# The chosen experts' DRAM round trip, by halves: own writes, reads and semaphores in a mixture-of-experts chain

## The reference

```python
x = x + L0(x)   # top 2 of 8 experts per batch: (gelu(x Wg) * (x Wu)) Wd, 256 -> 1024 -> 256,
                # weighted by the renormalised softmax, plus one shared expert of the same form
x = x + L1(x)   # x times a mix of 8 masked 256x256 matrices, mixed per batch, plus bias
x = x + L2(x)   # base matrix plus rank-16 terms of 8 experts
x = x + L3(x)   # the one argmax expert per batch: (silu(x Wu + b) * (x Wg + b)) Wd + b
```

## Time and profile before

| what | value |
|---|---|
| median of 3 runs | 1282.7 us (1278.59 to 1284.48) |
| the profiled execution's own time | 1279.28 us |
| its span in the trace | 1277.7 us |
| mean granted clock of TensorE | 0.965 |
| busy: PE / DVE / ACT / POOL | 1157.5 / 719.9 / 431.1 / 466.0 us |
| DMA | 245.07 MB in 267302 packets, mean 192 GB/s |

### The profile page before, as it was taken

One profiled execution on the slowest core, in us unless ns is written; L12 is line 12 of the kernel. 1 busy time (PEld: TensorE's weight loads), 2 busy tenths in 40 slices (PEclk: granted clock), 3 DMA queues, 4 the chain that ended last, 5 costly groups with the idle time before them and its releaser, 6 DMA issues.

```text
span 1277.7 us, 24975 instructions
## 1 busy us (share of the span) xinstructions
PE 1157.5 (91%) x6894; PEld 971.0 (76%) x6895; DVE 719.9 (56%) x1255; ACT 431.1 (34%) x845; POOL 466.0 (36%) x296
## 2 busy tenths in 40 slices
PE   8999997987967998797987797998999999899998
PEld 7999985775755776665765576787999999788776
DVE  6766675546646557465564555654555655544443
ACT  4456521322312222222322222232223223366664
POOL 2377686007126018044080636201000000688750
PEclk9999999998989999899998999998999999899999
DMA  7288858567666657657676677555655546576753
GB/s 215 72 281 300 310 149 276 160 208 195 169 209 191 198 180 208 208 162 240 188 209 200 181 211 221 160 165 151 177 145 143 136 130 192 176 251 217 216 165 106
DMA packets 267302, 245.07 MB, mean 192 GB/s; under 512 B 79936, under 2 KB 241984, under 8 KB 265152
## 3 DMA queue, kind: packets, MB, share of 16 engines
q1 hardware_dynamic: 253520, 193.95, 50.3%
q0 software_dynamic: 13680, 49.81, 13.2%
HBM read 176.59 MB, written 67.11 MB: 191 GB/s over the span
## 4 chain that ended last, share of the span: by engine, by line
PE 52%; DMA 22%; SPq 9%; DVE 7%; issue 6%; ACT 2%; POOL 1%; DVEq 0%; ACTq 0%; POOLq 0%
DMA squares<-acc 11%; DMA routing<-squares 10%; PE bank L765 7%; PE bank L766 7%; PE bank L767 7%; PE bank L1199 6%; DVE RS L1835 3%; PE bank L1228 3%; PE bank L855 3%; SPq L314 2%; PE bank L1043 2%; PE bank L906 2%; PE bank L908 2%; PE bank L1177 2%; PE bank L907 2%
## 5 line engine op out<-in xcount | busy, mean ns | idle before, releaser
L611 POOL TENSOR_TENSOR W<-raw,one 128x1024 fp32r<-128x1024 f32 x79 | 150.5, 1905 | 649.3 <-DVE acc L1902 354.4
L765 PE MATMUL bank<-W,RS 128*128 (+1 forms) x512 | 214.0, 418 | 54.7 <-DVE RS L1795 52.3
L855 PE MATMUL bank<-W,RS 128*128 x480 | 186.4, 411 | 39.7 <-DVE RS L1835 39.3
L766 PE MATMUL bank<-W,RS 128*128 (+1 forms) x512 | 208.4, 407 | 0.0
L1289 ACT ACTIVATE FS<-bank 128x512 f32<-128x512 f32 (+1 forms) x200 | 115.2, 576 | 274.2 <-PE bank L767 244.5
L767 PE MATMUL bank<-W,RS 128*128 (+1 forms) x512 | 207.5, 405 | 0.0
L613 POOL TENSOR_TENSOR W<-raw,W 128x1024 fp32r<-128x1024 f32 x79 | 195.3, 2472 | 6.2
L1835 DVE TENSOR_TENSOR RS<-routing,RS 128x512 fp32r<-128x512 f32 x120 | 123.7, 1068 | 85.8 <-ACT RS L1303 85.3
L765 PEld LDWEIGHTS bank<-W,RS 128*128 128x128 f32 x512 | 101.2, 198 | 86.5 <-issue 65.5
L1303 ACT ACTIVATE RS<-routing 128x512 fp32r<-128x512 f32 x120 | 70.3, 625 | 236.0 <-DMA routing<-squares 226.6
L855 PEld LDWEIGHTS bank<-W,RS 128*128 128x128 f32 x480 | 91.7, 191 | 71.9 <-issue 57.6
(11 more groups left out here) (236 smaller groups left out, 2072.5 us busy)
## 6 DMA issues: line engine op xcount, KB each, us to landing
raw<-in_w POOLq DMA_DIRECT2D x87, 512.0 KB, 4.8
acc<-in_w SPq DMA_DIRECT2D x70, 512.0 KB, 5.3
routing<-squares SPq DMA_DIRECT2D x60, 512.0 KB, 3.9
mixes<-acc SPq DMA_DIRECT2D x16, 1024.0 KB, 6.3
W<-mixes SPq DMA_DIRECT2D x16, 1024.0 KB, 6.1
squares<-X SPq DMA_DIRECT2D x60, 256.0 KB, 3.5
squares<-acc SPq DMA_DIRECT2D x60, 256.0 KB, 3.5
FS<-in_xT SPq DMA_DIRECT2D x200, 64.0 KB, 3.0
```

The lines of the kernel that those rows point to most:

```text
L611: pool.tensor_tensor(hi, raw[:, k, :], ones_like(PIECE), ALU.mult).then_inc(done, 1)
L765: pe.matmul(ps, ah, bh, start=(i == 0), stop=False)
L766: pe.matmul(ps, ah, bl, start=False, stop=False)
L855: mm = pe.matmul(both, chunk(hh[h], c), w2_, start=(h == 0 and c == 0), stop=(h == 1 and c == 3))
```

## The change

The tensor `squares` gets a place for each half, and `hidT` becomes two tiles' worth of columns, one for each half. Each half has its own write, its own read, and its own semaphores `square_out[h]` and `hidT_in[h]`. The transpose (s, h) waits for the write (s-1, h) alone. Nothing else is computed, and the same bytes travel.

SyncE's order in step s becomes: x for s+2; write (s, 0); read (s-1, 1); the mixed group's weights where there are any; write (s, 1); read (s, 0); the store of s-2. ScalarE takes the high part (s-1, 0) ahead of gelu (s, 1), and (s-1, 1) behind it. VectorE takes the low part (s-1, 0) ahead of hidden (s, 1), and (s-1, 1) at the end, behind the add. At the end of the stage TensorE does down (67, 1) one shared quarter later.

```diff
-    squares = nc.dram_tensor("squares", (2, P, I0), F32, kind="Internal").ap()
+    squares = nc.dram_tensor("squares", (2, 2, P, I0 // 2), F32, kind="Internal").ap()
...
-        hidT = routing[:, 0:I0]
+        hidT = [routing[:, I0 // 2 * h:I0 // 2 * (h + 1)] for h in range(2)]
...
+            def write_square(s, p, h, at):
+
+                n = P if at.half is None else S
+                sp.wait_ge(squared, 2 * s + h + 1)
+                sp.dma_start(squares[p, h].rearrange("p (g x) -> p g x", g=4)[:, :, 0:n],
+                             square[h][:, 0:4 * n].rearrange("p (g x) -> p g x", g=4)).then_inc(square_out[h], 16)
+
+            def read_hidT(s, p, h, at):
+
+                n = P if at.half is None else S
+                sp.wait_ge(square_out[h], 16 * s + 16)
+                sp.dma_start(hidT[h].rearrange("p (a x) -> p a x", a=4)[:, :, 0:n],
+                             squares[p, h].rearrange("(a i) (g x) -> (i g) a x", a=4, g=4)[:, :, 0:n])\
+                    .then_inc(hidT_in[h], 16)
...
             with sp.Fori(0, NMIXED0) as m:
                 for k in range(BODY):
-                    s, at = 2 + BODY * m + k, place_at(m, k - 2)
-                    if at.half != 0:
-                        load_skill(S0 + s + 2, k % 2, place_at(m, k + 2))
+                    s, p = 2 + BODY * m + k, k % 2
+                    at, before = place_at(m, k), place_at(m, k - 1)
+                    load_skill(S0 + s + 2, p, place_at(m, k + 2))
+                    write_square(s, p, 0, at)
+                    read_hidT(s - 1, 1 - p, 1, before)
                     if k < 2:
                         load_mixed0(m, 0, ((0, 1, 2, 3), (4, 5))[k], S0 + BODY * m)
                     if k in (HALVES[0] + 3, HALVES[0] + 4):
                         load_mixed0(m, 1, ((0, 1, 2, 3), (4, 5))[k - HALVES[0] - 3], S0 + BODY * m + HALVES[0] + 3)
-                    write_squares(s, k % 2, place_at(m, k))
-                    if at.half != 0:
-                        store_chosen(S0 + s - 2, k % 2, at)
-                    else:
-                        load_skill(S0 + s + 2, k % 2, place_at(m, k + 2), added=S0 + s - 1)
-                    read_hidT(s, k % 2, place_at(m, k))
+                    write_square(s, p, 1, at)
+                    read_hidT(s, p, 0, at)
+                    if place_at(m, k - 2).half != 0:
+                        store_chosen(S0 + s - 2, p, place_at(m, k - 2))
...
-            for q in range(2):
-                up_gate_late(0, 0, q)
-                last = load_expert_at(NR0 - 2 + q)
-                for h in range(2):
-                    down_chosen(NR0 - 2 + q, h, last)
+            up_gate_late(0, 0, 0)
+            last = load_expert_at(NR0 - 2)
+            for h in range(2):
+                down_chosen(NR0 - 2, h, last)
+            up_gate_late(0, 0, 1)
+            last = load_expert_at(NR0 - 1)
+            down_chosen(NR0 - 1, 0, last)
             up_gate_late(0, 0, 2)
+            down_chosen(NR0 - 1, 1, last)
...
-                act.wait_ge(hidT_in, 16 * s + 16)
+                act.wait_ge(hidT_in[h], 16 * s + 16)
...
+                if before_at is not None:
+                    hidden_hi_chosen(s - 1, 0, before_at)
                 gelu(1, 2 * g + 1, n=n)
                 if before_at is not None:
-                    for h in range(2):
-                        hidden_hi_chosen(s - 1, h, before_at)
+                    hidden_hi_chosen(s - 1, 1, before_at)
...
                 if not (isinstance(s, int) and s == 0):
-                    dve.wait_ge(squares_out, 32 * s)
+                    dve.wait_ge(square_out[h], 16 * s)
...
+                if before_at is not None:
+                    hidden_lo_chosen(s - 1, 0, before_at)
                 hidden_chosen(s, 1, at)
                 hidden_squares(s, 1, at)
...
-                for h in range(2):
-                    hidden_lo_chosen(s - 1, h, before_at)
                 if add_at is not None:
                     add(g - 2, p, add_at)
+                hidden_lo_chosen(s - 1, 1, before_at)
```

More of the change, by code:

```diff
@@ L252, in build @@
         hh_done, hl_done = sem("hh_done"), sem("hl_done")
-        squared, squares_out, hidT_in = sem("squared"), sem("squares_out"), sem("hidT_in")
+        squared = sem("squared")
+        square_out = [sem(f"square_out{h}") for h in range(2)]
+        hidT_in = [sem(f"hidT_in{h}") for h in range(2)]
         down_done, acc_done, add_step = sem("down_done"), sem("acc_done"), sem("add_step")
@@ L297, in turned_hid @@
         def turned_hid(h):
-            return hidT.rearrange("p (a h k t) -> p h k a t", a=4, h=2, k=4)[:, h]
+            return hidT[h].rearrange("p (a k t) -> p k a t", a=4, k=4)
         def turned_mixed(h, c):
-            return hidT.rearrange("p (a y) -> p a y", a=4)[:, :, S * h + 32 * c:S * h + 32 * (c + 1)]
+            return hidT[h].rearrange("p (a x) -> p a x", a=4)[:, :, 32 * c:32 * (c + 1)]
         block = ctx.enter_context(nc.Block())
@@ L363, in load_shared, with load_skill @@
                 home_x(g - 2)
-            def load_skill(g, p, at, added=None):
+            def load_skill(g, p, at):
                 slot = 2 * at.full if at.half is None else 2 * FULL0 + 2 * at.mixed
                 batches = table_values(sp, source[0:1, bass.ds(slot, 2)], NB - 1)
-                if added is None:
-                    sp.wait_ge(xl_done, g - 1)
-                else:
-                    sp.wait_ge(acc_done, added)
+                sp.wait_ge(xl_done, g - 1)
                 load_x(g, p, batches)
@@ L418, in _ @@
             spill(WPIECES - 1)
-            def write_squares(s, p, at):
-                n = D if at.half is None else P
-                for h in range(2):
[L423 to L435, removed]
+            def write_square(s, p, h, at):
[3 more added lines that the diff above has]
+                             square[h][:, 0:4 * n].rearrange("p (g x) -> p g x", g=4)).then_inc(square_out[h], 16)
@@ L437, in _ @@
+            def read_hidT(s, p, h, at):
[4 more added lines that the diff above has]
+                    .then_inc(hidT_in[h], 16)
             for k in range(NSTAGE):
                 sp.wait_ge(spilled[k], 16 * WPIECES // NSTAGE)
-            write_squares(0, 0, FIRST_TWO[0])
@@ L440, in _ @@
             load_skill(S0 + 2, 0, place_at(0, 0))
-            read_hidT(0, 0, FIRST_TWO[0])
+            write_square(0, 0, 0, FIRST_TWO[0])
+            write_square(0, 0, 1, FIRST_TWO[0])
+            read_hidT(0, 0, 0, FIRST_TWO[0])
             load_skill(S0 + 3, 1, place_at(0, 1))
-            write_squares(1, 1, FIRST_TWO[1])
-            read_hidT(1, 1, FIRST_TWO[1])
+            write_square(1, 1, 0, FIRST_TWO[1])
+            read_hidT(0, 0, 1, FIRST_TWO[0])
+            write_square(1, 1, 1, FIRST_TWO[1])
@@ L445, in _ @@
+            read_hidT(1, 1, 0, FIRST_TWO[1])
             with sp.Fori(0, NMIXED0) as m:
                 for k in range(BODY):
-                    s, at = 2 + BODY * m + k, place_at(m, k - 2)
-                    if at.half != 0:
-                        load_skill(S0 + s + 2, k % 2, place_at(m, k + 2))
+                    s, p = 2 + BODY * m + k, k % 2
[3 more added lines that the diff above has]
+                    read_hidT(s - 1, 1 - p, 1, before)
@@ L453, in _, with load_late @@
                         load_mixed0(m, 1, ((0, 1, 2, 3), (4, 5))[k - HALVES[0] - 3], S0 + BODY * m + HALVES[0] + 3)
-                    write_squares(s, k % 2, place_at(m, k))
-                    if at.half != 0:
-                        store_chosen(S0 + s - 2, k % 2, at)
-                    else:
-                        load_skill(S0 + s + 2, k % 2, place_at(m, k + 2), added=S0 + s - 1)
-                    read_hidT(s, k % 2, place_at(m, k))
-            def load_late(t):
-                for k in range(2):
+                    write_square(s, p, 1, at)
+                    read_hidT(s, p, 0, at)
+                    if place_at(m, k - 2).half != 0:
+                        store_chosen(S0 + s - 2, p, place_at(m, k - 2))
+            def load_late(t, ks=(0, 1)):
+                for k in ks:
                     sp.wait_ge(xl_done, S1 + 2 * t + k - 1)
@@ L470, in store_x3 @@
                              x3out.rearrange("p (t d) -> p t d", t=2)).then_inc(x3_stored, 16)
-            load_late(0)
-            write_squares(NR0 - 2, 0, LAST_TWO[0])
-            store_chosen(S1 - 4, 0, place(NR0 - 4))
-            read_hidT(NR0 - 2, 0, LAST_TWO[0])
-            write_squares(NR0 - 1, 1, LAST_TWO[1])
+            load_late(0, (0,))
+            write_square(NR0 - 2, 0, 0, LAST_TWO[0])
+            read_hidT(NR0 - 3, 1, 1, place(NR0 - 3))
+            write_square(NR0 - 2, 0, 1, LAST_TWO[0])
+            read_hidT(NR0 - 2, 0, 0, LAST_TWO[0])
+            store_chosen(S1 - 4, 0, place(NR0 - 4))
+            load_late(0, (1,))
+            write_square(NR0 - 1, 1, 0, LAST_TWO[1])
+            read_hidT(NR0 - 2, 0, 1, LAST_TWO[0])
```

(13 more changed lines are left out.)

## The result

The changed kernel takes 1201.1 us (median; 1199.4 to 1204.1) against 1280.8 for the kernel before in the same runs: ratio 0.938, 95% interval 0.935 to 0.941, 6.2% faster. The forecast was 1205.

The account below looks back on a forecast made before the run. TensorE and the write-read round trip through DRAM were taken as nearly equal bounds, every disturbance paid at once. 39 + 24 + 6 + 15 - 8 = 76 us off 1279.3, plus half of 3.4, gave 1205; range 1172 to 1250.

Parts of the forecast that it names:

- term 2: Chosen stage, separate half reads: TensorE's waits for the returned low half fall from 38.7 to 15, gaining 24 us.
- The 8 us: Taken off the gain for VectorE's slowed subtractions, now in front of hidden (s, 1); bounds 0 and 20 us.
- term 1: Chosen stage, own write semaphores and queue order: waits for the split of x fall from 51.5 to 12, gaining 39 us.
- Removes all but the long ones: Waits for the split of x average 3.0 us; a shift of up to 4.15 leaves only long ones.
- that leaves 3: Both half reads gain 3.3 to 4.15 us, leaving 3 us of low-half waits before 12 from mixed loads.
- Term 3: Mixed groups' 6.8 us of waits before their matmuls, from the same DRAM trip; gain 6 us.
- Term 4: TensorE's clock: of 34 us of full speed not granted, 22 fall on matmuls, two thirds return; gain 15 us.
- Price of a half read: A 256 KB half read in 512-byte runs takes 3.7 us, against 3.9 for the whole.
- Queue time: SyncE's one extra read a step costs 0.38 us of issue, covered at under 6 in 8.3; uncovered 26 us.
- D: Slower: half reads over 6.5 us, with shorter, doubled runs, lengthen half 0's loop; at 7.0, 1308 us; chance 0.08.
- C: Nothing changes: read (s, 0) still queues for write (s, 1), savings hidden; within 6 us of 1281; chance 0.05.
- B: Half the gain: order couples the halves and slow reads eat the slack, or mixed loads' bytes decide; 1243; chance 0.25.

## Why the prediction was right, point by point

- **The time**, 1205 against 1201, is inside the range. The mechanism that I gave for it is only in part the one that the runs show, and the sum is right by luck. It forecast 76 us and the span lost 78.4, but term 2 was 19 too high (24 against 38.7 - 34.1 = 4.6). The 8 us not lost on VectorE, 6 more from the busy time, 5 behind the stage that are in no term, and 3 more in term 1 made up for it.
- **What bounds the kernel.** The trip and TensorE nearly equal, every disturbance paid at once: right. The loop was read wrongly. I closed it through the landing of the write, from the step at 630.55, one of those where the queue waited for it. The queue waits 83.1 us there and 162.9 at the store for the add. Two steps that I did not cost follow from it: that the add moves ahead of the late low part, and that the read of half 1 no longer stands behind the store of the same step. The add's move decides: without it 77 us are gone. The second was not tested by itself.
- **Term 1**, 51.5 to 12, measured 9.1. Its size was right and its cause not sufficient: own semaphores alone bring nothing (1.003), and in the changed kernel they are worth 25 us. "Removes all but the long ones" failed in the kernel before, where the queue's wait at the store stayed (170.2 us against 162.9).
- **Term 2**, 38.7 to 15, measured 34.1. The failed step is "that leaves 3": I took each old wait and subtracted the new slack. The four loop starts cost 2.9, 3.7, 5.9 and 5.5 us, 18 in place of 12. Another 16 us remain in 15 waits elsewhere: one of 3.2 in the middle of a round, which I had at nothing, and 14 of 0.9 us on average. The mechanism named for the loop starts, read (s, 0) behind 2 MB, was right, and its size short: at the third round's start it landed at 492.96, 12.1 us after the first piece in place of about 10.
- **Term 3**, 6.8 to nothing, measured 0.8.
- **Term 4**, 15 us of clock, measured 17.3, and 20.8 with the rest of TensorE's busy time. The share was right: 17.3 of 27.9 us is 62%, where I had two thirds. What I undercounted was the loss on matmuls, 22 for 27.9 us.
- **The 8 us** set aside for slowed subtractions on VectorE: waits and busy time of TensorE together give 73 us of the stage's 73.2, so nothing of the kind shows beside them. The subtractions took 1087 ns on average against 1068 before; what they cost is inside the waits.
- **Price of a half read**: 3.7 taken, 3.2 measured in the changed kernel. By the Trainium skill (DMA: Bandwidth & Descriptors, Anatomy of one DMA) the estimate is 2.6; its fit was measured on transfers that GpSimd issues, and these are SyncE's. The measured 3.2 lies between. **Queue time**: covered, as said; two reads in place of one cost 4 us on the kernel before.
- **Rivals.** D would have needed half reads over 6.5 us; they took 3.2. (Its price was a slip: at 7.0 us the step is 0.5 us over, not 0.4, which makes 34 us and 1315.) Its other leg, the Trainium skill's rule to batch transfers (DMA: Bandwidth & Descriptors, Bandwidth), is answered by the two half reads alone: some 4 us. C did not happen, but its time is what this change gives with the add left where it stood, 1278, for another reason than C's. B asked for the coupling of halves by order: that is the true danger of this kernel, but through the add and the store. B's sign did show at loop starts: the late copy of half 0 ran at 492.98 and its gelu only behind it, at 493.51. But in the whole stage VectorE waited 8.2 us for gelus, against 54.6 before, so it stayed small.
- **What would show it**: stage 611 us (about 610 said), L771 waits 9.1 (under 15), a transpose waiting for a write in none of VectorE's waits (under 30), mean clock 0.989 over the span (0.97 or more), all met; a half read took 3.2, not 3.7. Waits on L861 near 15 and only at four loop starts: wrong, 34.1 in 19.

## What to carry to other kernels

When a change rewrites the order of several in-order engines, cost each moved operation by who stands behind it: ask what the DMA queue itself waits for, since a store that waits for a late add holds up every load behind it. An operation placed behind one that waits for a transfer puts the transfer into every loop that passes through it. Parts of such a change are not additive: semaphores worth nothing alone were worth 25 us in the changed kernel, so test each part by removing it from the whole as well as by adding it alone.

## What the runs showed of the hardware that was not expected

- With 512 runs of 512 bytes in a 256 KB write to DRAM in place of 128 runs of 2048, in otherwise equal kernels, the time of the whole grew by 11 us. Halving the mixed groups' reads gave no shorter landing: 128 KB in 256-byte runs took 3.8 us, 256 KB in 512-byte runs 3.7 before.
- A read of 256 KB that was issued behind four loads of 512 KB on the same queue landed after 9.3 us in place of 3.2.
- A loop's end on SyncE showed 3.4 to 4.0 us without an issue, and writing the loop out gained 16 us over four rounds. How much of it is the loop's end itself, and how much other costs of the loop, no run separated.
- A kernel can be slow at a high granted clock. With the add behind the late half TensorE waited 106 us in the stage, in 85 pieces of at most 3.4, against 98 in 46 of up to 8.4 in the kernel before, and was busy 580.5 us against 586.5. The two kernels take the same time, at a mean clock of 0.986 and 0.965.
- In slices of 1 us the stage's clock was under 0.9 in 15 stretches in the kernel before, in 7 with the add behind the late half, and in 5 in the changed kernel, most of them about 4 us long. The five of the changed kernel lie at or right behind its five waits of 2.9 to 5.9 us, at 209, 349, 495, 561 and 645 us. This is no rule for other kernels: in the kernel before a wait of 1.8 us, at 442, was followed by such a stretch too. The matmuls behind the longest of the five:

```profile
494.70:500.50 5.80, 5.75 (x16) 4.73 (x17) 4.13 (x9) 2.20 (x5) 0.00 (x0) 0.53 0.73 256
```

Not tried: moving the add alone in the kernel before, with one read and the old queue order, where the read would have to wait for the low parts by itself. So the runs show that the add's move is needed, and not how much it would bring alone.
